# Graph attention over 16 images on one core: another order of the work in a slot on ScalarE, VectorE and TensorE, and immediate biases

## What is computed

```python
alpha = relu(bn(einsum('bchw,oc->bohw', x, wa)))     # query, 32 channels
sigma = relu(bn(einsum('bchw,oc->bohw', x, ws)))     # key, 32 channels
att = softmax(where(adj, einsum('bkn,bkm->bnm', af, sf), NEG))   # 8 neighbours of a pixel
h_s = einsum('bnm,bcm->bcn', att, xf)
Gc = einsum('bcn,bdn->bcd', xf, xf)
catt = softmax(where(cadj, Gc, NEG))                  # 2 neighbours of a channel
h_p = einsum('bcd,bdn->bcn', catt, xf)
out = (1 - gama) * x + gama * elu(h_s + h_p)
```

## Time and profile before

| what | us |
|---|---|
| median of 3 runs | 604.75 |
| lowest and highest run | 601.31, 605.41 |
| the profiled execution, its own time | 608.46 |
| its span, first to last instruction | 606.7 |
| mean granted TensorE clock in it | 0.904 of full speed |

### The profile page before, as it was taken

One profiled execution on the slowest core, in us unless ns is written; L12 is line 12 of the kernel. 1 busy time (PEld: TensorE's weight loads), 2 busy tenths in 40 slices (PEclk: granted clock), 3 DMA queues, 4 the chain that ended last, 5 costly groups with the idle time before them and its releaser, 6 DMA issues.

```text
span 606.7 us, 18825 instructions
## 1 busy us (share of the span) xinstructions
PE 492.1 (81%) x7621; PEld 385.8 (64%) x7684; DVE 380.1 (63%) x669; ACT 429.2 (71%) x1043; POOL 233.9 (39%) x140
## 2 busy tenths in 40 slices
PE   0468989888898888979798888989798997888783
PEld 0236677666767575767667575767667686675672
DVE  3213576665857666675857676675857676584872
ACT  0244678758877777858777777868877777787683
POOL 5200044334424442444334442444334442443365
PEclk9995997979899898979999898979999797889877
DMA  8990055765666567655766567655767477523113
GB/s 234 241 244 15 3 169 145 210 191 154 179 190 191 165 188 209 199 168 166 199 179 193 161 200 209 193 178 166 196 190 208 126 210 204 178 87 124 71 71 139
DMA packets 55702, 102.28 MB, mean 169 GB/s; under 512 B 6208, under 2 KB 6464, under 8 KB 55616
## 3 DMA queue, kind: packets, MB, share of 16 engines
q1 hardware_dynamic: 55616, 101.07, 58.0%
HBM read 34.20 MB, written 33.55 MB: 112 GB/s over the span
## 4 chain that ended last, share of the span: by engine, by line
PE 49%; DVE 24%; issue 13%; ACT 12%; DMA 2%; SPq 1%; POOLq 0%; DVEq 0%; ACTq 0%
PE z L439 17%; PE gb L439 13%; DVE z L361 9%; PE xp L449 8%; PE score L439 7%; ACT probs L263 5%; DVE gram_d L385 4%; PE et L525 4%; ACT z L278 3%; DVE neg_max L339 3%; DVE gram_e L380 2%; ACT upper L235 2%; DMA const<-constants_dram 2%; DVE probs_t L354 1%; DVE probs L346 1%
## 5 line engine op out<-in xcount | busy, mean ns | idle before, releaser
L214 POOL TENSOR_TENSOR blend<-elu,blend 128x1024 f32<-128x1024 f32 x64 | 150.8, 2356 | 360.7 <-ACT elu L290 360.7
L439 PEld LDWEIGHTS z<-probs_t,upper 64*128 64x128 f32 x2304 | 165.1, 201 | 76.5 <-issue 75.1
L439 PE MATMUL z<-probs_t,upper 64*128 64x128 f32 (+1 forms) x2304 | 182.6, 295 | 36.1 <-DVE z L361 34.1
L449 PE MATMUL xp<-const,x 128*128 128x128 f32 x512 | 94.9, 314 | 44.7 <-ACT upper L235 37.6
L361 DVE SCALAR_TENSOR_TENSOR z<-near,catt,z 128x512 f32<-128x512 f32 x128 | 91.8, 752 | 61.8 <-ACT z L278 61.7
L263 ACT ACTIVATE probs<-score,neg_max 128x128 f32<-128x128 f32 x256 | 90.5, 371 | 55.2 <-DVE neg_max L339 55.2
L278 ACT ACTIVATE z<-x,vec,catt 128x512 f32<-128x512 f32 x128 | 94.6, 773 | 10.2 <-DVE catt L393 9.9
L235 ACT ACTIVATE upper<-xp 128x512 f32<-128x512 f32 x128 | 76.0, 594 | 32.3 <-PE xp L449 28.4
L449 PEld LDWEIGHTS xp<-const,x 128*128 128x128 f32 x512 | 62.1, 157 | 57.5 <-issue 50.7
L366 DVE SCALAR_TENSOR_TENSOR elu<-elu,z 128x512 f32<-128x512 f32 x128 | 81.8, 680 | 14.7 <-ACT elu L285 14.7
L439 PE MATMUL score<-key,query 32*64 32x64 f32 (+1 forms) x1536 | 78.3, 247 | 13.9 <-issue 5.8
(11 more groups left out here) (49 smaller groups left out, 253.5 us busy)
## 6 DMA issues: line engine op xcount, KB each, us to landing
x<-x_dram SPq DMA_DIRECT2D x64, 512.0 KB, 6.2
out_dram<-blend SPq DMA_DIRECT2D x64, 512.0 KB, 4.1
near<-x SPq DMA_DIRECT2D x128, 224.0 KB, 5.0
near<-x SPq DMA_DIRECT2D x128, 30.0 KB, 4.6
const<-constants_dram SPq DMA_DIRECT2D x1, 435.5 KB, 10.2
const<-constants_dram SPq DMA_DIRECT2D x1, 128.0 KB, 2.1
wt<-w_dram SPq DMA_DIRECT2D x1, 64.0 KB, 3.4
vec<-vectors_dram SPq DMA_DIRECT2D x1, 5.5 KB, 3.1
```

The lines of the kernel that those rows point to most:

```text
L214: nc.gpsimd.tensor_tensor(blend[s % BLENDS][:, :, :], elu[s % 2][:, :, :], blend[s % BLENDS][:, :, :], ALU.add).then_inc(blend_done, 1)
L439: return nc.tensor.matmul(o, l, r, start=start, stop=stop, skip_group_check=True, **kw)
L449: last = nc.tensor.transpose(xp[:, v * C + h * P:v * C + (h + 1) * P], xb[:, h, at0:at0 + WIN], ident)
```

## The change

Four things change. The instructions are the same in number on every engine.

- ACT: in a slot both `exp_z` come first, then the first `move_xt`, then `move_query` or `move_key`, then `times_gama` and `exp_gram`; only then `exp_scores`, the second `move_xt`, `move_halo`, and the two `weigh_own` last.
- DVE: `elu_out` comes first, then `gram_softmax_in`, `maxima`, `move_probs`, `gram_softmax_out`, `gram_pick`, `normalise`, and the two `mix_channels` last as before.
- PE: `project_query` goes from slot 2 to slot 1, `project_key` from slot 3 to slot 2, and `edges` from behind the second `z_sums` of slot 3 to ahead of it.
- The biases 1 and -1 of `weigh_own` and `exp_z`, which were read from columns of `vec`, are given as numbers; `vec` is two columns narrower.

```diff
@@ weigh_own, exp_z
-                                     scale=catt[:, h, 1 - h:2 - h], bias=vec[:, V_ONE:V_ONE + 1]).then_inc(product_done, 1)
+                                     scale=catt[:, h, 1 - h:2 - h], bias=1.0).then_inc(product_done, 1)
-                nc.scalar.activation(elu[s % 2][:, h, :], z[s % 2][h][:, :], ACT.Exp, bias=vec[:, V_MINUS:V_MINUS + 1])\
+                nc.scalar.activation(elu[s % 2][:, h, :], z[s % 2][h][:, :], ACT.Exp, bias=-1.0)\
@@ the loop over the slots on ACT
-                if b + 1 < B:
-                    move_xt(b + 1, q, 0)
                 for h in range(HALF):
                     if real(t - 3):
                         exp_z(t - 3, h)
+                if b + 1 < B:
+                    move_xt(b + 1, q, 0)
+                if q == 2 and b + 1 < B:
+                    move_query(b + 1)
+                if q == 3 and b + 1 < B:
+                    move_key(b + 1)
+                if real(t - 3):
+                    times_gama(t - 3)
+                if q == 1 and 0 <= b < B:
+                    exp_gram(b)
                 if real(t):
                     exp_scores(t)
                 if b + 1 < B:
                     move_xt(b + 1, q, 1)
-                if q == 1 and 0 <= b < B:
-                    exp_gram(b)
-                if q == 2 and b + 1 < B:
-                    move_query(b + 1)
                 if q == 3 and b + 1 < B:
-                    move_key(b + 1)
+                    move_halo(b + 1)
                 for h in range(HALF):
                     if real(t - 1):
                         weigh_own(t - 1, h)
-                if real(t - 3):
-                    times_gama(t - 3)
-                if q == 3 and b + 1 < B:
-                    move_halo(b + 1)
@@ the loop on DVE
+                for h in range(HALF):
+                    if real(t - 3):
+                        elu_out(t - 3, h)
                 if q == 1 and 0 <= b < B:
                     gram_softmax_in(b)
                 if real(t):
                     maxima(t)
-                for h in range(HALF):
-                    if real(t - 3):
-                        elu_out(t - 3, h)
+                if real(t - 1):
+                    move_probs(t - 1)
                 if q == 1 and 0 <= b < B:
                     gram_softmax_out(b)
+                if q == 0 and 0 <= b < B:
+                    gram_pick(b)
                 if real(t):
                     normalise(t)
-                if q == 0 and 0 <= b < B:
-                    gram_pick(b)
-                if real(t - 1):
-                    move_probs(t - 1)
@@ the loop on PE
-                if q == 2 and b + 1 < B:
+                if q == 1 and b + 1 < B:
                     if b < 0:
                         pe.wait_ge(const_in, 48)
                     project_query(b + 1)
+                if q == 2 and b + 1 < B:
+                    project_key(b + 1)
                 if q == 3 and b + 1 < B:
-                    project_key(b + 1)
+                    edges(b + 1)
                 if real(t - 2):
                     z_sums(t - 2, 1)
                 if q == 0 and 0 <= b < B:
                     shift_gram(b)
-                if q == 3 and b + 1 < B:
-                    edges(b + 1)
```

More of the change, by code:

```diff
@@ L35 @@
 C_ALL = C_MASK + MASKS
-V_GAMA, V_ONE, V_MINUS = 8, 9, 10
+V_GAMA = 8
 def graph_attention(nc, x, w_t, vectors, constants, out):
@@ L68, in graph_attention @@
         wt = sb("wt", [P, HALF, 2 * HID])
-        vec = sb("vec", [P, 11])
+        vec = sb("vec", [P, 9])
         bn = sb("bn", [P, 8, 2])
@@ L623 @@
     norms = np.stack([a[n + s] for s in "as" for n in "gbmv"], axis=1)
-    vectors = np.concatenate([np.tile(norms, (QUARTERS, 1)), np.tile(a["gama"].reshape(1, 1), (P, 1)),
-                              np.tile(np.array([[1.0, -1.0]], np.float32), (P, 1))], axis=1)
+    vectors = np.concatenate([np.tile(norms, (QUARTERS, 1)), np.tile(a["gama"].reshape(1, 1), (P, 1))], axis=1)
     arrays = {"x_dram": a["x"], "w_dram": w_t, "vectors_dram": vectors, "constants_dram": shape_constants()}
```

## The result

The changed kernel took 595.0 us (median of 4 runs, 583.7 to 611.7) beside 605.1 before. Its runs fall in two groups, 583.7 and 586.3 us at granted clocks of 0.887 and 0.902, and 603.8 and 611.7 us at 0.868 and 0.849; ratios compare the faster group alone, and here the ratio is 0.968, with a 95% interval of 0.959 to 0.976. Timed again on another chip (run e1) it took 597.8 against 606.6, ratio 0.988 (0.982 to 0.994); one of these six runs took 1446 us and is not in the ratio. So it gains one to three per cent. I had forecast 556 with a range of 538 to 592: the sign was right and the size was missed by some 40 us.

The account below looks back on a forecast made before the run. It took a ring of engines waiting for each other, 34.5 us an image, as the bound. Slots of 8.0, 6.8, 6.9 and 9.5 us made 31.2, saving 3.3 over 15 periods: 556 us forecast, range 538 to 592.

Parts of the forecast that it names:

- The ring and its beat: No engine fills the 34.5 us image period; engines wait in a ring, timed by the end of each slot's second mix.
- slots 1 to 3: Three of an image's four slots, forecast at 8.0, 6.8 and 6.9 us in place of 9.4, 9.0 and 7.4.
- ACT's wait for the query: ACT waiting for the query projection, 41.4 us in 16 waits before; forecast to be near nothing.
- DVE and POOL shut each other out: Claim that some DVE instructions and POOL's cannot run together, so L346 ends 0.54 us behind a POOL instruction.
- `catt` stalled: In slot 1, `catt` was forecast to meet POOL's L214 and take about 2 us in many images.
- rival B: In slot 1 `catt` is not shut out by POOL: period 30.0 us, 538 us in all; chance 0.08.
- rival C: POOL keeps the way from L214 to L208, so L346 ends later: period 33.9 us, 596 in all; chance 0.08.
- Slot 0. This one is PE's: PE's 6.08 us from first sums to `et` transposes, then DVE's work: 9.5 us in place of 8.7.
- The change, slot by slot: The step that counted each slot between ends of last mixes: 31.2 us an image in place of 34.5.
- rival A: The clock falls once in slot 0, costing 1.8 us: period 33.0 us, 582 in all; chance 0.12.
- rival D: The clock stays low over slot 0's whole PE path, 4.9 us more: 629 us in all; chance 0.10.
- The sign that I had set for both: A PE clock below 0.9 with low windows behind the start of slot 0, for rival A and rival D.

Follow-up runs that it names:

- e2: The changed kernel with slot 0's transfers held back until `gram_band` is done; 561.1 us, ratio 0.927.
- e14: The changed kernel with slot 0's transfers held until `gram_band` is done and six idle mask matmuls before slot 0's first sums; 537.5 us, ratio 0.896.
- e11: The kernel before with only PE's new places for projections and edges, the early query and key copies, and immediate biases; 547.3 us, ratio 0.902.
- e8: The kernel before with only PE's new places for projections and edges and the early query and key copies on ACT; 554.0 us, ratio 0.915.
- e9: The changed kernel with `times_gama` put back behind `weigh_own` at the end of ACT's slot; 562.0 us, ratio 0.927.
- e13: The kernel before with slot 0's loads and copies issued in slot 3, ahead of its store; 619.2 us, ratio 1.035.
- e5: The changed kernel with `gram_band` cut from 17 groups to 2; 570.4 us, ratio 0.942.
- e4: The changed kernel with six idle mask matmuls in PE's rest before the sums of slot 0; 586.3 us, ratio 0.965.

## Why the prediction was wrong

**What held.** The ring and its beat: slots 1 to 3 came within 0.1 us, in this image and in the medians of the trace. `gram_d` fell from up to 2.37 to 0.16, and ACT's wait for the query went. DVE and POOL shut each other out where I had put it: L346 at 295.61 ended at 297.04, 0.55 behind L214 (294.11 + 2.38), and in slot 1 L346 (288.69 + 1.57) ended 0.53 behind L208 (288.54 + 1.19). L208 was shut out in its turn: 1.63 us in slot 3 in place of 1.20. `catt` stalled in 13 of 16 images, 1.04 us here and up to 1.62, less than the 2 that I had, because it begins later in L214's run; its end is what counts, and it ended with L214, at 288.57. That also settles rival B, and rival C: the waiting DVE instruction had its turn between L214 and L208.

**What failed.** The step "Slot 0. This one is PE's", where I took 6.08 us from the trace of before "with the clock up" and moved it as it was. It measured 8.99 in the image shown, and the whole slot 12.45 (11.9 in the mean) in place of 9.5. Two things were in that term and neither is constant. A gap of 0.71 us without a releaser was inside it, and I had seen no reason for it to grow; it became 2.67, as the change brought the transfers forward onto `gram_band`. In "The change, slot by slot" I had counted what gama's earlier place does to POOL and DVE, but not what POOL's earlier end releases: the store, and with it every transfer that SP holds behind it. And I took the clock as up because a rest of 0.69 had been followed by sums at full speed; the rest that I myself forecast at 1.6 was longer, and the row for such a rest, 1.50 us with sums of 1.76 behind it, was there in the earlier trace rows. That was rival A, to which I gave 0.12; where the whole path ran at 0.50, as from 408 and 442 us, it was rival D (0.10), but it cost up to 2.9 us over my 9.5, not 4.9. The sign that I had set for both, a clock below 0.9, came: 0.894.

**How they add up.** My forecast for the profiled execution was 559: 15 periods of 31.2 us and the rest as before. Between its first and last `catt` e1 measured 503.0 us, so periods of 33.5: 35 us more, and the execution took 592.9. In e2 the periods are 32.4, still 18 us too much over 15 images, but its head and tail are 10 us shorter than those of before, because the gap at the first `gram_band` and the low clock behind it are gone; that gives 566.4. So it is partly luck that e2's median of 561 lies near my 556. In e14 the periods are 30.3 and the execution took 535.5. That its periods fall below my 31.2 fits: my 9.5 for slot 0 held the 0.71 gap, and slot 0 measured 8.6. From e1 to e14 the two losses together are 60 us in the medians and 57 in the profiled executions; how they share it is less firm, 36.7 and 23.5 by the medians, 26.5 and 30.9 by the profiled executions.

**A term left open.** I had put the biases at nothing. They brought 6.8 us in e11, but in e8's order, where by my slot sums ACT arrives last in two slots. In the changed order I did not try them alone, so no run says whether nothing was right there.

**How far the causes are shown.** That a gap without a releaser is PE without instructions rests on this: it ends 1.2 to 1.7 us behind the end of an instruction packet, every time, and it begins at one fixed place in the count by 256 of PE's instructions (e1); it goes when the transfers move away (e2, e9) and comes when they move in (e13); it goes when `gram_band` has 240 instructions fewer (e5); and the page lists the queue of these packets on the same DMA engines, 61 of them in e1:

```profile
q8 instruction: 61, 1.00, 0.7%
```

That the packets come late because of the transfers is shown by e2 and e13, which move only transfers. Where in the DMA engines they wait is not: the trace has the start and end of a packet, not the moment at which it was asked for. That the low clock follows PE's rest before the sums is shown by e4 and e14, which only fill that rest; why some rests are followed by it and others, like that of 305.41, are not, stays open.

## What to carry to other kernels

When an edit makes an engine finish earlier, follow what that releases down to the DMA queue, and look what the transfers will then lie on. A stretch of many short matmuls is the wrong place for a burst of data, and where a gap has no releaser, the instruction packets of the trace are worth setting beside it. A gap without a releaser in a term of a sum is a term of its own, and so is the clock behind each rest that the sum forecasts. And a change of several parts is worth taking apart even where it gains: here one part brought 50 us and the rest gave 44 back.

## What the runs showed of the hardware

PE's instructions came in packets of 16 KB, 256 instructions each, through a queue of the DMA engines. When data was issued ahead of a run of 136 short matmuls, a packet could come late, and PE stood for up to 3 us in the images and 4.9 us in the head (e1); when the same data was issued behind that run, such waits were 0.2 us in `gb` and 1.3 us in all (e2). PE went on 1.16 to 1.72 us behind the end of the packet. Less work on PE can lower its clock: e5 took some 20 us of matmuls away (15 of 17 parts of 1.49 us, 16 times), and its clock was 0.865, against 0.894 with them. Six matmuls an image that compute nothing bought 23.5 us, once the instructions came in time (e14).
